# A causal attention stage with cheaper row masks and another rule for its filler products, and the last expert's further-block loop put behind the last scatter-adds

## The reference

```
x = x + moe_gated(group_norm(x))      # 8 experts, 2 per token, 256 -> 1024 -> 256, silu(x w1) * (x w3) w2
t = t + attention(layer_norm(t))      # causal, 16 heads of 16 channels, scale 1/16, softmax, bias, Wo
t = t + moe(layer_norm(t))            # 8 experts, 2 per token, 256 -> 512 -> 256, exact gelu
```

## Time and profile before

| | |
|---|---|
| Time, median of 3 runs | 638.2 us (637.08 to 638.49) |
| The profiled execution: own time | 643.67 us |
| its span, first to last instruction | 642.1 us |
| mean granted TensorE clock | 0.897 |
| busy: PE, DVE, ACT, POOL | 86%, 63%, 43%, 33% of the span |
| attention's scores, values and projection | from 289 to 490 us |
| last gather-add instruction on GpSimd starts | 630.8 us |

### The profile page before, as it was taken

One profiled execution on the slowest core, in us unless ns is written; L12 is line 12 of the kernel. 1 busy time (PEld: TensorE's weight loads), 2 busy tenths in 40 slices (PEclk: granted clock), 3 DMA queues, 4 the chain that ended last, 5 costly groups with the idle time before them and its releaser, 6 DMA issues.

```text
span 642.1 us, 10995 instructions
## 1 busy us (share of the span) xinstructions
PE 553.6 (86%) x3740; PEld 405.9 (63%) x3741; DVE 406.4 (63%) x998; ACT 277.3 (43%) x656; POOL 210.1 (33%) x233
## 2 busy tenths in 40 slices
PE   5789999999999990698999989999999799899930
PEld 2478999999998980376444444544435378788830
DVE  3688878878877841944654766748115677876610
ACT  2434454444445412140213747556454056576730
POOL 5240513405312202965000330202010256776531
PEclk9689999999999995796675989969699799999975
DMA  8864735645565106149100140000002356676721
GB/s 314 278 177 143 194 108 149 199 148 149 153 192 125 15 12 150 34 81 195 22 0 2 22 81 3 2 2 1 2 1 102 121 144 153 143 158 167 159 28 17
DMA packets 49422, 66.49 MB, mean 104 GB/s; under 512 B 6017, under 2 KB 37249, under 8 KB 49345
## 3 DMA queue, kind: packets, MB, share of 16 engines
q1 hardware_dynamic: 37936, 48.46, 24.6%
q0 software_dynamic: 11424, 17.25, 15.2%
HBM read 46.62 MB, written 13.70 MB: 94 GB/s over the span
## 4 chain that ended last, share of the span: by engine, by line
PE 64%; DVE 13%; DMA 6%; issue 5%; ACT 4%; SPq 2%; POOLq 1%; POOL 1%; DVEq 1%; ACTq 0%
PE banks L772 18%; PE banks L843 9%; PE banks L1105 6%; PE banks L1076 6%; PE banks L847 5%; PE banks L1013 4%; PE banks L1006 4%; DVE w_lo L1400 2%; DVE hot L1393 2%; DMA got<-rows,from_row 2%; PE banks L827 2%; PE banks L1088 2%; ACT gated_y L1220 1%; SPq L491 1%; PE banks L1131 1%
## 5 line engine op out<-in xcount | busy, mean ns | idle before, releaser
L1289 ACT ACTIVATE probs<-banks 128x512 f32<-128x512 f32 (+3 forms) x192 | 83.5, 490 | 103.3 <-PE banks L1076 97.9
L1664 DVE TENSOR_REDUCE maxes<-banks 128x2 f32<-128x1024 f32 (+2 forms) x96 | 89.1, 956 | 38.7 <-PE banks L1013 19.5
L1400 DVE TENSOR_TENSOR w_lo<-stage,w_hi 128x512 fp32r<-128x512 f32 (+1 forms) x200 | 90.9, 504 | 21.1 <-ACT w_hi L1164 20.3
L1164 ACT ACTIVATE w_hi<-stage 128x512 fp32r<-128x512 f32 (+1 forms) x200 | 83.6, 485 | 3.6 <-DMA stage<-in_w 3.6
L772 PE MATMUL banks<-xg_hi,w_hi 128*128 128x320 f32 (+2 forms) x328 | 81.1, 328 | 3.2 <-issue 1.8
L843 PE MATMUL banks<-w_hi,a_hi 128*128 128x256 f32 (+1 forms) x296 | 78.4, 295 | 6.0 <-DVE a_hi L1498 5.0
L715 POOL DMA_INDIRECT res<-gated_y,to_row x24 | 37.8, 1574 | 139.1 <-ACT gated_y L1220 114.5
L772 PE MATMUL banks<-xg_lo,w_hi 128*128 128x320 f32 (+2 forms) x328 | 76.7, 315 | 0.0
L772 PE MATMUL banks<-xg_hi,w_lo 128*128 128x320 f32 (+2 forms) x328 | 76.7, 315 | 0.0
L843 PE MATMUL banks<-w_lo,a_hi 128*128 128x256 f32 (+1 forms) x296 | 73.6, 278 | 0.0
L760 POOL TENSOR_SCALAR_AFFINE_SELECT probs<-probs 128x512 f32<-128x512 f32 x32 | 20.3, 635 | 156.7 <-ACT probs L1289 156.7
(11 more groups left out here) (194 smaller groups left out, 827.6 us busy)
## 6 DMA issues: line engine op xcount, KB each, us to landing
stage<-in_w SPq DMA_DIRECT2D x48, 512.0 KB, 5.9
stage<-in_ffn_w SPq DMA_DIRECT2D x36, 256.0 KB, 3.7
rows<-rows SPq DMA_DIRECT2D x2, 1056.0 KB, 5.7
rows<-rows SPq DMA_DIRECT2D x2, 1024.0 KB, 5.8
q_st<-qk_hi SPq DMA_DIRECT2D x32, 64.0 KB, 5.2
k_st<-qk_hi POOLq DMA_DIRECT2D x32, 64.0 KB, 4.8
xT<-in_xT SPq DMA_DIRECT2D x2, 512.0 KB, 4.5
tok<-res SPq DMA_DIRECT2D x2, 512.0 KB, 4.4
```

The costliest lines, as they stand in the source:

```text
L1164: ins = act.activation(dst, src, ACT.Copy)
L1289: act.activation(probs_of(u, step)[:, j, c0:HALF], exp_bank[n % EXP_BANKS][:, c0:HALF], ACT.Exp, scale=float(C) ** -0.5).then_inc(by_scala ...
L1400: ins = dve.tensor_tensor(lo, src, f32(hi), ALU.subtract)
L1664: dve.tensor_reduce(maxes[:, u % 2, 2 * pr:2 * pr + 2, i % QT, c], out[:, :].rearrange("p (h t) -> p h t", h=2)[:, :, 0:w], AX_X, ALU.max) ...
```

## The change

There are three parts.

**Masks.** `row_mask` is one product of 128 columns in bfloat16 for each head, the identity against the triangle alone, put on the 128 diagonal columns. `ident_r` and `mask_r` become `ident_b` and `mask_b`.

**Planner.** `run_until` counts how much of the last `WINDOW` = 3.4 us PE has streamed, by the columns of the pieces planned, and puts in fills until that is `SHARE` = 0.6 of it, also where there is no pause, from 14.5 us of plan time on. Fills now take plan time (0.1 us and 0.213 us each) and count as streamed. The cost of a masked rows piece goes from 0.55 to 0.23 us beside its scores, that of a values piece from 0.12 to 0.22. The stacks are taken to be there at 16, 26 and 34 us in place of 14, 22 and 30, and those of the second pair of heads of unit 0 seven us later.

**The last pass of L1.** On GpSimd the last pass of L1 issues its adds first, and then runs the loop over further blocks and raises `all_added`. A further block would wait for all adds. L0 keeps its order.

```
+WINDOW, SHARE, KEEP, KEEP_FROM = 3.4, 0.6, HALF / 2400, 14.5
...
     def run_until(start):
         nonlocal pe
-        n = int((start - pe - 0.2) / 0.22)
+        n = int((start - pe - 0.2) / KEEP)
+        past = sum(min(t, end - pe + WINDOW) for end, t in streamed if end > pe - WINDOW)
+        n = max(n, math.ceil((SHARE * WINDOW - past) / KEEP) if pe > KEEP_FROM else 0)
         if n > 1:
             order.append(("keep", n, summing, len(pv_ends)))
+            pe += 0.1 + n * KEEP
+            streamed.append((pe, n * KEEP))
         pe = max(pe, start)
...
-    stack_at = {0: 14.0, 1: 22.0, 2: 30.0}
+    stack_at = {0: 16.0, 1: 26.0, 2: 34.0}
...
-            on_vector(("rows", u, pr, i, c), stack_at[g], (0.55 if c == qb else 0.1) + max(w, 2 * P) / 2400,
-                      0.16 + 2 * w / 960)
+            on_vector(("rows", u, pr, i, c), stack_at[g] + (7.0 if u == 0 and pr else 0.0),
+                      (0.23 if c == qb else 0.1) + max(w, 2 * P) / 2400, 0.16 + 2 * w / 960,
+                      max(w, 2 * P) + (2 * P if c == qb else 0))
...
             run_until(start)
-            pe += 0.12 + 4 * w / 2400
+            runs(0.22 + 4 * w / 2400, 4 * w)
...
-                if e == last:
-                    pool.wait_ge(ran_ready, 1 + (not m.gated))
-                    pool.wait_ge(s["wlo_done"], m.passes * m.nf)
-                    further_blocks(pool, m, lambda e, b, q: further(m, rows_d, res_d, e, q))
-                    pool.sem_inc(s["all_added"], 1)
+                if e == last and m.gated:
+                    all_further()
                 pool.wait_ge(s["to_ready"], e + 1)
                 pool.wait_ge(s["gy_ready"], e + 2)
                 pool.sem_inc(dma_go, 1)
...
                                             ).then_inc(s["added"], 16)
+                if e == last and not m.gated:
+                    all_further()
...
-        pool.tensor_copy(ident_r[:, :], ident[:, :])
-        link(pool.memset(mask_r[:, :].bitcast(F32), 0.0))
-        tri = mask_r[:, P:2 * P]
-        pool.affine_select(out=tri, in_=tri.bitcast(F32), compare_op=ALU.is_ge, fill=MASKED, base=0, pattern=[[-1, P]],
-                           channel_multiplier=1).then_inc(cleared, 1)
+        pool.tensor_copy(ident_b[:, :], ident[:, :])
+        link(pool.memset(mask_b[:, :], 0.0))
+        pool.affine_select(out=mask_b[:, :], in_=mask_b[:, :], compare_op=ALU.is_ge, fill=MASKED, base=0,
+                           pattern=[[-1, P]], channel_multiplier=1).then_inc(cleared, 1)
...
             d = (i % QT) * P
-            first, cols = (0, mask_r[:, P:3 * P]) if d == 0 else (d - P, mask_r[:, 0:2 * P])
-            return pe.matmul(out[:, first:first + 2 * P], ident_r[:, :], cols, start=False, stop=True,
+            return pe.matmul(out[:, d:d + P], ident_b[:, :], mask_b[:, :], start=False, stop=True,
                              skip_group_check=True)
```

More of the change, by code:

```diff
@@ L20 @@
+import math
 from contextlib import ExitStack
@@ L103, in attention_order, with runs, on_vector @@
     summing = False
+    streamed = []
     def run_until(start):
         nonlocal pe
-        n = int((start - pe - 0.2) / 0.22)
+        n = int((start - pe - 0.2) / KEEP)
+        past = sum(min(t, end - pe + WINDOW) for end, t in streamed if end > pe - WINDOW)
+        n = max(n, math.ceil((SHARE * WINDOW - past) / KEEP) if pe > KEEP_FROM else 0)
         if n > 1:
             order.append(("keep", n, summing, len(pv_ends)))
+            pe += 0.1 + n * KEEP
+            streamed.append((pe, n * KEEP))
         pe = max(pe, start)
-    def on_vector(piece, ready, mine, its):
+    def runs(t, columns):
+        nonlocal pe
+        pe += t
+        streamed.append((pe, columns / 2400))
+    def on_vector(piece, ready, mine, its, columns=HALF):
         nonlocal pe, vector, n_vector
         run_until(max(ready, vector_free[n_vector % TURN_SLOTS]))
-        pe += mine
+        runs(mine, columns)
         vector = max(vector, pe + 0.15) + its
@@ L127, in attention_order @@
     for piece in values[:QT]:
-        on_vector(piece, 0.0, 0.75, 0.45)
+        on_vector(piece, 0.0, 0.75, 0.45, 6 * C)
     left = values[QT:]
-    stack_at = {0: 14.0, 1: 22.0, 2: 30.0}
+    stack_at = {0: 16.0, 1: 26.0, 2: 34.0}
     rows = [(u, pr, i, c) for u, (g, qb) in enumerate(UNITS) for pr in range(2)
@@ L145, in attention_order @@
         if rows and UNITS[rows[0][0]][0] in stack_at:
-            picks.append((max(pe, stack_at[UNITS[rows[0][0]][0]], slot), "rows"))
+            picks.append((max(pe, stack_at[UNITS[rows[0][0]][0]] + (7.0 if rows[0][:2] == (0, 1) else 0.0), slot),
+                          "rows"))
         if waiting:
@@ L154, in attention_order @@
             w = min(HALF, (i + 1) * P - c * HALF)
-            on_vector(("rows", u, pr, i, c), stack_at[g], (0.55 if c == qb else 0.1) + max(w, 2 * P) / 2400,
-                      0.16 + 2 * w / 960)
+            on_vector(("rows", u, pr, i, c), stack_at[g] + (7.0 if u == 0 and pr else 0.0),
+                      (0.23 if c == qb else 0.1) + max(w, 2 * P) / 2400, 0.16 + 2 * w / 960,
+                      max(w, 2 * P) + (2 * P if c == qb else 0))
             if left and len(order) % 3 == 0:
-                on_vector(left.pop(0), 0.0, 0.75, 0.45)
+                on_vector(left.pop(0), 0.0, 0.75, 0.45, 6 * C)
             if pr == 1 and i % QT == QT - 1 and c == qb:
@@ L168, in attention_order @@
             run_until(start)
-            pe += 0.1 + max(w, 2 * P) / 2400
+            runs(0.1 + max(w, 2 * P) / 2400, max(w, 2 * P))
             if pr == 0:
@@ L206, in attention_order @@
             if piece[0] == "maxrow":
-                done = on_vector(piece, at, 0.55, 0.75)
+                done = on_vector(piece, at, 0.55, 0.75, 8 * P)
                 order.append(("maxdma", u))
@@ L210, in attention_order @@
             elif piece[0] == "out":
-                done = on_vector(piece, at, 0.55, 0.85)
+                done = on_vector(piece, at, 0.55, 0.85, 8 * P)
                 if UNITS[u][0] == GROUPS - 1:
@@ L218, in attention_order @@
             else:
-                on_vector(piece, at, 0.55, 0.9)
+                on_vector(piece, at, 0.55, 0.9, 4 * C)
     return order
@@ L364, in build @@
     probs2 = in_experts("probs2", [P, HG, HALF], F32)
-    ident_r = in_experts("ident_r", [P, P], F32R)
-    mask_r = in_experts("mask_r", [P, 3 * P], F32R)
+    ident_b = in_experts("ident_b", [P, P], BF16)
+    mask_b = in_experts("mask_b", [P, P], BF16)
     max_rows = in_experts("max_rows", [P, 2, HALF], F32)
@@ L683, in further @@
             pool.wait_ge(s["o_gy_ready"], q + 1)
+            if not m.gated:
+                pool.wait_ge(s["added"], 16 * NT * E + m.moved(E))
             pool.sem_inc(dma_go, 1)
@@ L699, in former_added, with all_further @@
                 pool.sem_inc(s["gy_free"], 1)
+            def all_further():
+                pool.wait_ge(ran_ready, 1 + (not m.gated))
+                pool.wait_ge(s["wlo_done"], m.passes * m.nf)
+                further_blocks(pool, m, lambda e, b, q: further(m, rows_d, res_d, e, q))
+                pool.sem_inc(s["all_added"], 1)
             def expert(e, par):
```

## The result

The changed kernel takes 633.67 us, median of 18 executions, where the kernel before takes 638.04, median of 18. The ratio is 0.992 with a 95% interval of 0.9893 to 0.9946: 5 us faster, and far short of the 25 us that were forecast. The profiled execution has a span of 631.1 us and a granted clock of 0.92.

A forecast was written before the change was run, and what follows sets the result against it. PE was taken to bound the kernel (64% of the chain), with 67.5 us of attention at half clock. Masks -7, clock -20, fills +8, stacks +2, tail -8 gave -25 us, from 638.2 to 613; 8-in-10 range 601 to 634.

The forecast's parts named there:

- the clock's -20: Attention on PE: fills give back two thirds of 30 us lost at half clock, 20 us, leaving 22 us at half clock.
- the tail's -8: Program end: GpSimd's end instruction waits for something of the last adds, so issuing them earlier gains 8 us.
- Masks, -7: Attention's 64 mask pairs: 0.20 us each instead of 0.44, 15 us of PE, of which 7 us on the path.
- The second reading: Program end: the end instruction's 9.4 us are its own and begin when GpSimd's queue is empty, a gain of 3 us.
- Fills, +8: Attention on PE: 68 more fills in 20 more places, about half taken by pauses, cost 8 us on the path.
- stacks, +2: Attention's unit 0: later planned stack times put the second pair's fills past today's wait, costing 2 us more.
- What the planner can't see: Attention: the rule doesn't see the 1.08 us PE stop at 372 us, and thinner masks thin the stretches holding the clock.
- the fills buy nothing: Rival, attention: fills stream where the clock stays at half anyway and cost 10 us, up to 19; 633 us; chance 0.11.
- Partly held: Rival, attention: 34 us at half clock stay, 15 us come back; 620 us, or 623 with tail at 5; chance 0.20.
- Slower: Rival, attention's long stretch 376.5 to 417.5 us and its twin: thinner masks let the clock fall; 645 us; chance 0.07.
- the mean clock: Sign, whole span: the mean granted clock goes from 0.90 to about 0.93.
- the end instruction: Sign, program end: a GpSimd end instruction that still lasts 12 us would show the forecast wrong.

The follow-up runs named there:

- e_masks: The kernel before with only the change to 16-bit masks of 128 columns, old order and fills: median 634.4 us, ratio 0.996.
- e_tail: The kernel before with only the last pass's adds issued ahead of the loop over further blocks: median 640.6 us, ratio 1.000.
- e_again: The changed kernel run once more, unaltered: median 634.1 us, ratio 0.990 to the kernel before.
- e_early: The changed kernel with the last layer's loop ahead of the adds of the last pass but one: median 635.8 us, ratio 0.989 to the kernel before.
- e_gate: The changed kernel with one test that skips the loop over further blocks, all engines, both layers: median 617.4 us, ratio 0.970 to the kernel before.
- e_same: The kernel before run once more, unchanged: median 639.2 us, ratio 0.998.
- e_best: The changed kernel with loops skipped by a test, group 3's stack DMAs deferred, old stack times, no counted share: 612.1 us, 0.958 of the kernel before.
- e_share0: The changed kernel with the counted share set to 0, fills in planned pauses only: median 631.3 us, ratio 0.985 to the kernel before.
- e_plan: The kernel before with only the planner's change (order, fills, stack times, costs), old float32r masks: median 634.2 us, ratio 0.993.
- e_stack: The changed kernel with the planner's old stack times (14, 22, 30): median 631.8 us, ratio 0.983 to the kernel before.
- e_defer: The changed kernel with GpSimd's group 3 stack DMAs moved ahead of the masking of unit 2's last values piece: 634.3 us, 0.984 of the kernel before.

## Why the prediction was wrong, point by point

The sign was right, and the time, 633.7, lies at the upper edge of a range that reached to 634; but 25 us were forecast and 5 came. Two steps failed and make most of the 20 us between: the clock's -20 was mis-sized (8 to 11 measured), and the tail's -8 rested on a wrong wait (1 measured). Term by term:

- **Masks, -7.** Right at full clock: a pair takes 0.21 us (0.20 taken), and the attention is 7.4 us shorter. In whole executions e_masks is 2.5 us faster (0 to 5), and some of the rest went back through the clock. That thin masks thin the stretches was said, but priced at nothing of its own.
- **The tail, -8.** Wrong. The step that failed is the one on what GpSimd's end instruction waits for: I took it to wait for something of the adds, since the same instruction is short on other engines. It takes 9.5 us from an empty queue, whatever was before. Also the loop, run while the adds are made, took 10.0 us in place of 8.1. Measured: -1.0 in the profile, nothing in e_tail's time. The second reading, "a gain of 3", had the mechanism, and its 3 become 1 with the longer loop. The Trainium skill's load of freshly loaded code ("GPSIMD Engine Reference", 2.1 Instruction dispatch), cited beside it, isn't shown to be the cause; no run tells what the 9.5 us are made of.
- **Clock, -20.** Mis-sized twice. The cure was 24 us of half clock on average, not 45: the one profile of before stood high (68 us in the attention, where two more profiles of the same order have 51 and 58), and the forecast's 22 left over stood low (24 in the first profile of the new attention, but 41, 34 and 31 in e_again, e_early and e_gate). Of what stays, the stop behind GpSimd's DMAs brings some 10 us, and the thin masks perhaps 11. And the price of 0.45 us for each is the top of what was seen: between e_same and the profile of before it is 7.1 us for 17, 0.42; between the changed kernel's two profiles 5.1 for 17, 0.30. A straight line through time against half clock, over all executions with one offset for each kernel, has a slope of 0.34. So 24 us at 0.34 to 0.45 are 8 to 11 us.
- **Fills, +8, and stacks, +2.** Too low by 1 to 4 us or about right, by the price of the clock: the order alone adds 14 us (193.9 against 180.1 for e_masks, both at full clock; 11 with e_again), but 9 to 10 if half clock is taken off at 0.34. The share rule is 3 to 5 of it, the stop behind GpSimd's DMAs some 2 to 4, since the new order stretches it from 1.1 to 3.0 us; the stack times 0 to 2. The rest may be the fills in planned pauses, 92 in place of 42, or the changed sequence of the pieces; e_best, without the three parts named, still has 184.7 against 180.1, and no run separates what is left.
- **What the planner can't see.** The stop of the earlier trace rows was read as one "with nothing that the profile shows", and I only feared for the clock there. Its cause, GpSimd's queue, would have been visible: the masking stands behind the DMAs at 371.45 in the rows shown above.

Sum: masks -7, order +11 to +14, clock -11, tail -1 at a price of 0.45 is -5 to -8 us; at 0.34 it is masks -7, order +9 to +10, clock -8, tail -1, -6 to -7 us. Measured are 5 (3 to 7 by the interval). The order's term is found by subtraction between single profiles, so this sum is a fair account and no proof.

Two numbers of the rivals don't follow from their own terms: 638.2 - 20 is 618, not 620 (621, not 623, with the tail at 5), and 641 holds the masks' -7 already, so 637 would count part of them twice.

Of the rivals, *the fills buy nothing* came nearest in its time (633), and e_share0 bears it out for the counted share, though not for all fills: half clock did fall by 24 us. *Partly held* (620) had the half clock that stays about right (34 us), and its worth (15) and the tail wrong. *Slower*, with the clock falling in the long stretch, didn't happen: in the changed kernel the clock stays up from 383.5 to 480, in e_again from 376. Its cause, thin masks that cost clock, has some support in the mean clocks above, at a smaller size. Whether the transposes pull the clock down no run here tells apart from the stops beside them, so the Trainium skill's rule on them ("TensorE: Matmul & The Clock Gate", Part 4: PE-mode transpose) stays open too.

Of the signs, the mean clock is 0.92 (0.93 forecast), the end instruction lasts 9.5 us and not 12, and from the landing of the last pass but one to the end of the span it is 21.2 us where some 14 were forecast.

Open: four of the ten profiles with the new order (changed, e_plan, e_share0, e_stack) show 14 us at half clock inside the last layer, e_defer 10, the others 7 like all with the old order. Whether the order has to do with it wasn't tried.

## What to carry to other kernels

A filler's price can lie on the path each time (3 to 5 us for the counted ones here), while what it gives back is a clock that varies by 17 us of half clock from one profile to the next: price it against several profiles of the kernel before, not one. A planner that orders one engine must know the other engines' queues too; here twelve DMA issues of 0.48 us on GpSimd ahead of a 0.65 us masking stopped PE for 3 us, with a fall of the clock behind it, at a place where the planner had put just two fills. And before moving a loop that does nothing, look whether one test can skip it: that was worth 13 us by the ratios of e_gate and e_again (17 by their medians on one chip), with both layers' loops. At the last layer's end alone it was 7 us, where moving the loop was worth one.

## What the runs showed of the hardware that I had not expected

- GpSimd's end instruction takes 9.5 us from an empty queue in all fourteen profiles: 9.47 us with the last add 7 us back (changed kernel, e_tail), and the span ends 9.7 to 10.0 us behind the last add's record where that is last (before, e_early, e_gate). On PE, ACT, VectorE and SyncE it takes 8 to 66 ns.
- A loop of eight empty turns costs 8.1 us on GpSimd's sequencer alone, 10.0 while it also issues adds, and 15 on PE's (607.6 to 622.6 in the changed kernel).
- The same program has 51 to 68 us of half clock in its attention, and 7 us of time hang on that.
- A stop of PE of 1.8 to 3.2 us in the attention was followed by a fall of the granted clock to half within 4 us in eight profiles of eight, for 3.4 to 20.5 us; stops of 1.3 to 1.5 us were followed by one in some profiles (311 in e_again) and not in others (311 in the changed kernel).
